# Two cross-attentions on one Trainium2 core: ScalarE rounds a key after it normalises probabilities instead of before

## The reference, cut to what matters

```python
def _cross_attention(q_in, kv_in, wq, bq, wk, bk, wv, bv, wo, bo, bias_k, bias_v):
    qh = (q_in @ wq + bq).reshape(b, q_len, H, K)          # 16 heads of 128
    kh = (kv_in @ wk + bk).reshape(b, t, H, K)
    vh = (kv_in @ wv + bv).reshape(b, t, H, K)
    kh = jnp.concatenate([kh, jnp.broadcast_to(bias_k, (b, 1, H, K))], axis=1)
    vh = jnp.concatenate([vh, jnp.broadcast_to(bias_v, (b, 1, H, K))], axis=1)
    logits = jnp.einsum('bqhk,bthk->bhqt', qh, kh) / jnp.sqrt(K)
    weights = jax.nn.softmax(logits, axis=-1)
    ctx = jnp.einsum('bhqt,bthk->bqhk', weights, vh).reshape(b, q_len, H * K)
    return ctx @ wo + bo
```

## Time and profile before

| | |
|---|---|
| median of 3 runs | 2650.89 us (2647.5 to 2654.44) |
| the profiled execution: its time, its span | 2650.34 us, 2648.6 us |
| PE busy | 2456.9 us, 93% of the span |
| PEld busy | 2163.3 us, 82% |
| DVE busy | 1382.3 us, 52% |
| ACT busy | 1133.2 us, 43% |
| POOL busy | 871.7 us, 33% |
| mean granted TensorE clock | 0.956 |

### The profile page before, as it was taken

One profiled execution on the slowest core, in us unless ns is written; L12 is line 12 of the kernel. 1 busy time (PEld: TensorE's weight loads), 2 busy tenths in 40 slices (PEclk: granted clock), 3 DMA queues, 4 the chain that ended last, 5 costly groups with the idle time before them and its releaser, 6 DMA issues. The chain is left out here.

```text
span 2648.6 us, 37894 instructions
## 1 busy us (share of the span) xinstructions
PE 2456.9 (93%) x13976; PEld 2163.3 (82%) x13976; DVE 1382.3 (52%) x2328; ACT 1133.2 (43%) x2441; POOL 871.7 (33%) x514
## 2 busy tenths in 40 slices
PE   7899689989999699899999999989998999999698
PEld 5676334479897467699999999989998999999698
DVE  4566631268886643232266666633335666664642
ACT  4677112123322332222476666622236566664320
POOL 1100322262210460252265454507216454542300
PEclk9899879989999699899999999999999999999799
DMA  7553263489995147344666655525266566653300
GB/s 234 128 137 72 77 220 113 113 246 229 249 235 183 68 158 242 120 157 155 203 220 201 196 188 176 172 74 208 106 228 218 167 198 199 198 186 107 123 9 25
DMA packets 196347, 432.94 MB, mean 163 GB/s; under 512 B 57820, under 2 KB 92660, under 8 KB 195396
## 3 DMA queue, kind: packets, MB, share of 16 engines
q1 hardware_dynamic: 196164, 430.52, 52.4%
HBM read 332.35 MB, written 106.27 MB: 166 GB/s over the span
## 5 line engine op out<-in xcount | busy, mean ns | idle before, releaser
L2008 PE MATMUL att_ring<-ca_pp,att_arena 128*128 128x400 f32 (+1 forms) x2304 | 431.3, 345 | 9.7 <-issue 7.5
L2008 PEld LDWEIGHTS att_ring<-ca_pp,att_arena 128*128 128x128 f32 (+1 forms) x2304 | 417.6, 189 | 16.0 <-issue 15.7
L2088 POOL TENSOR_TENSOR att_arena<-att_arena 128x1448 fp32r<-128x1448 f32 x64 | 212.2, 3316 | 471.8 <-ACT att_arena L2095 317.1
L2008 PE MATMUL att_ring<-att_arena,qk_wh 128*128 128x362 f32 x1024 | 256.0, 332 | 0.0
L2714 DVE TENSOR_TENSOR ca_yl<-att_ring,att_arena 128x400 fp32r<-128x400 f32 x256 | 146.7, 573 | 193.6 <-ACT att_arena L2675 193.6
L2008 PE MATMUL att_ring<-att_arena,qk_wl 128*128 128x362 f32 x512 | 173.0, 338 | 18.4 <-POOL att_arena L2275 17.8
L2008 PEld LDWEIGHTS att_ring<-att_arena,qk_wh 128*128 128x128 f32 x1024 | 185.3, 192 | 0.0
L2675 ACT ACTIVATE att_arena<-att_ring 128x400 fp32r<-128x400 f32 x256 | 129.0, 504 | 86.6 <-PE att_ring L2008 86.5
L2101 ACT ACTIVATE att_kstage<-att_score,att_shift 100x362 f32<-100x362 f32 x256 | 143.8, 563 | 43.4 <-DVE att_shift L2114 43.3
L1075 ACT ACTIVATE rec_stage<-rec_fbank,rec_columns 128x361 f32<-128x361 f32 x128 | 72.1, 564 | 196.4 <-PE rec_fbank L2008 195.6
L2008 PE MATMUL att_score<-att_arena 128*100 128x362 f32 x768 | 143.9, 337 | 0.8 <-POOL att_arena L2073 0.8
(11 more groups left out here) (410 smaller groups left out, 5898.4 us busy)
## 6 DMA issues: line engine op xcount, KB each, us to landing
att_arena<-ctx_parts SPq DMA_DIRECT2D x64, 1024.0 KB, 5.8
att_arena<-keys SPq DMA_DIRECT2D x64, 724.0 KB, 4.6
att_arena<-ctx_parts SPq DMA_DIRECT2D x64, 420.0 KB, 6.9
keys<-rec_stage SPq DMA_DIRECT2D x32, 724.0 KB, 4.2
keys<-att_kstage SPq DMA_DIRECT2D x32, 724.0 KB, 3.2
l_arena<-kept_value SPq DMA_DIRECT2D x176, 100.0 KB, 5.5
queries<-att_loose SPq DMA_DIRECT2D x64, 200.0 KB, 3.0
att_arena<-queries SPq DMA_DIRECT2D x64, 200.0 KB, 3.0
```

The lines of the kernel that those rows point to most:

```text
L2008: issued = nc.tensor.matmul(out, x, y, start=(first and k == 0), stop=(last and k == count - 1))
L2088: self.nc.gpsimd.tensor_tensor(self.kl[:, n % 2].bitcast(F32R), self.kl[:, n % 2], self.kh[:, n % 2].bitcast(F32), ALU.subtract).then_inc( ...
```

## The change

In each step ScalarE's four `normalise` of step n + 1 now stand ahead of `high_key(n + 3)`. Nothing is added or removed, and the lists of the other engines are as they were.

```diff
                 if n < STEPS:
                     for i in range(3):
                         turned_high(n, i)
-                if n + 3 < STEPS:
-                    t.high_key(act, n + 3)
                 if n + 1 < STEPS:
                     for h in range(G3):
                         t.normalise(act, n + 1, h)
+                if n + 3 < STEPS:
+                    t.high_key(act, n + 3)
                 j = half_due(n)
                 if j is not None:
```

## The result

The changed kernel takes 2671.01 us (median of 6 runs, 2667.57 to 2672.91) against 2650.61 us before (median of 6, those of the table above and three more). Its ratio to the kernel before is 1.0072, with a 95% interval of 1.0059 to 1.0084, so it is slower by some 19 us; the two medians differ by 20.4 us, the interval runs from 15.6 to 22.3 us. The forecast was 2667 us in a range of 2657 to 2673. The profiled execution took 2670.04 us, with a span of 2668.3 us and a mean granted clock of 0.956, as before.

What follows compares the result with a forecast made beforehand. TensorE's own list was taken to bound the steady part. 12.0 us from light steps and 4.4 us from the first steps made 16.4 us on 2650.34, 2666.7 us, forecast as 2667 us for the median, range 2657 to 2673.

Steps and rivals of the forecast that it cites:

- What bounds the kernel: Steady steps: TensorE's own list sets the pace; the split key and query lie ready only 2.02 us early.
- How much later the key comes: Light steps: key rounding starts 2.97 us later, against 2.02 us of slack, so the scores start 1.00 us late.
- How many steps: Steady part: 12 light steps over two attentions lose 1.00 us each, 12.0 us; the other steps cost nothing.
- The first four steps: Start of each attention, where DMAs are late: 2.2 us lost per attention, 4.4 us for both.
- Its larger term: Step 3 of the second attention: late key rounded 1.59 us later, 1.19 us lost; first attention taken as alike.
- The other term: Steps 0 to 2: GpSimd's weights split passes a net 1.0 us delay to step 2's key; bounds 0 and 1.5.
- step 1 starts earlier on ScalarE: Step 0's normalisation fits into ScalarE's idle time, so mixed contexts come 1.95 us earlier and step 1 starts earlier.
- The later mixed context costs nothing: Light step 7, ScalarE: first mixed context 1.02 us late, yet the exponential behind it could start at about 1412.03, before 1412.24.
- The clock: Rival: TensorE's clock falls in the 12 new gaps, 1.7 us each, 20 us more, 2687 us; chance 0.04.
- this rival's sign: The clock rival is decided by whether the scores behind the gap take over 3 us.
- The delay wasn't hidden: Rival: key rounding only 2 us later, light steps cost nothing, 2651 to 2655 us; chance 0.12.
- The gain by VectorE's earlier shift: Rival: shift 1.9 us sooner brings exponentials forward, 8 us gained, 2643 us; chance 0.03.

Runs made afterwards that it cites:

- e2: Kernel before, with normalising ahead of the key's rounding only in steps from n = 4 on that are not light; ratio 0.9994 (0.9983 to 1.0004).
- e4: Changed kernel, with GpSimd splitting the query ahead of the key; ratio to the kernel before 1.0001 (0.9992 to 1.0010).
- e5: Kernel before, with two of four normalisations ahead of the key's rounding; heads steps 18.98 or 18.99 us, one profiled execution 2656.89 us.
- e6: Kernel before, with three of four normalisations ahead of the key's rounding; heads steps 19.47 to 19.49 us, one profiled execution 2661.71 us.
- e3: Kernel before, with normalising ahead of the key's rounding only in steps 0 to 3 of each attention; ratio 1.0013 (1.0000 to 1.0027).
- e1: Kernel before, with normalising ahead of the key's rounding only in light steps n = 7, 11, ..., 27; ratio 1.0041 (1.0028 to 1.0055).

## Why the prediction was right

**What bounds the kernel.** Right. TensorE alone sets the pace of the steady steps, and the wait that came late was the one with the least slack, the split of key and query; e2 and e4 show it from both sides.

**How much later the key comes.** Right by each term: the normalisation starts 0.04 us behind the inversion's end (0.03 forecast), the rounding starts 2.98 us later in the step (2.97), and the scores 0.06 us behind the split's end (0.05). The loss for a heads step is 0.97 us where I had 1.00; the 2.98 less 2.02 of slack, plus the 0.06, would be 1.02, and the split itself was 0.05 us quicker than before (from 1416.25 to 1421.48, 5.23 us, against 5.28).

**How many steps.** Right: 12, and no others in the steady part, 11.6 us against 12.0. e5 and e6 show that the slack read from the rows was the real threshold.

**The first four steps.** The size, 4.4 us, is in line with e3 (3.4 us by the timing, 4.8 by means over profiles). Its larger term is borne out by the traces: step 3's late key was to cost 1.19 us, and the heads step behind it, step 4, lasts 20.18 us in the changed kernel's second attention and 20.19 us in both of e3, with TensorE idle for 0.97 us ahead of its scores. In the changed kernel's first attention step 4 lasts 19.83 us, and in the six attentions of the table where nothing is moved there 18.98 to 19.01. The other term, 1.0 us an attention in the steps ahead of it, is not shown: steps 0 to 3 together take 47.96 us as a mean of the four and 46.67 as a mean of the six, 1.3 us more, but they scatter by 1.9 us within the four and by 4.4 us within the six.

The working behind that second term held in part. Step 0 gets shorter, and TensorE gains nothing by it, as forecast: the scores of step 1 start 4.17 or 4.18 us into the step in the four attentions and 2.38 or 2.39 in the six, as they wait for GpSimd's split, which the earlier contexts don't bring forward. That "step 1 starts earlier on ScalarE" held in three attentions of four. Counted from TensorE's turning of step 0, ScalarE's first rounding of step 1 comes after 13.8 to 14.4 us in the first attentions where nothing is moved and 15.3 to 15.7 in the second ones; in e3 after 12.99 and 13.34, in the changed kernel after 14.52 and 14.54. The 14.52 is no gain, because there the rounding waits for the stacking of step 0's rows by DMA. ScalarE's timeline of that step:

```profile
1327.56 1.29 ACT L2669 ACTIVATE ca_pp<-att_ring 128x400 fp32r<-128x400 f32 x3 [1.93 <-DMA ca_extra<-ca_pp]
1329.75 2.06 ACT L2106 ACTIVATE att_kstage<-att_kstage,att_share 100x362 f32<-100x362 f32 x4 [0.90 <-DVE att_share L2119]
1331.72 1.40 ACT L2095 ACTIVATE att_arena<-att_arena 128x1448 fp32r<-128x1448 f32 x1
```

What ScalarE won by the reordering it spent here in waiting for that DMA, 1.93 us, so the key's rounding came 18.68 us behind the turning of step 0, where it was 14.96, and not 1.0 us later; the weights' split followed it. Two effects follow in this profile that my working didn't have. VectorE's shift of step 2 stood 4.35 us, under the weights' split, and ScalarE waited 2.37 us for it; the rows below are VectorE's, GpSimd's and ScalarE's of step 2. And SyncE's next stacking, which waits behind the same split, came late, so that ScalarE waited 2.69 us in step 3.

```profile
1342.42 4.35 DVE L2114 SCALAR_TENSOR_TENSOR att_shift<-att_top,att_zeros 100x4 f32<-100x4 f32 x1
```

```profile
1342.08 4.66 POOL L2649 TENSOR_TENSOR ca_wvl<-state_X,ca_wvh 128x2048 fp32r<-128x2048 f32 x1
```

```profile
1346.80 0.56 ACT L2101 ACTIVATE att_kstage<-att_score,att_shift 100x362 f32<-100x362 f32 x1 [2.37 <-DVE att_shift L2114]
```

Neither effect is shown to be the change's. In e1, which moves nothing in these steps, ScalarE waited longer still for the same shift, 6.01 us in step 2:

```profile
1340.91 6.96 DVE L2114 SCALAR_TENSOR_TENSOR att_shift<-att_top,att_zeros 100x4 f32<-100x4 f32 x1
```

```profile
1347.90 0.56 ACT L2101 ACTIVATE att_kstage<-att_score,att_shift 100x362 f32<-100x362 f32 x1 [6.01 <-DVE att_shift L2114]
```

And in e3's two attentions, which have the change in these steps, ScalarE doesn't wait for that shift in step 2; the wait for the stacking in step 3 is 1.91 and 1.46 us there, 1.32 us in the second attention before. How much of the loss each carries stays open.

**The later mixed context costs nothing.** Right: the exponential behind it starts 6.39 us into step 7 (1416.46 - 1410.07), before it was 6.60, and e2 has no loss in 38 steps that carry the same delay.

**The rivals.** The clock didn't fall in the 12 new gaps of the steady part: it is 1.00 in each of these heads steps. In the first steps it falls with and without the change: in step 1 it is 0.74 and 0.86 before and 0.88 and 0.78 after. One place there fits this rival's sign where it was 1.00 before. In step 3 of the first attention TensorE waits 1.94 us and the scores behind it take over 3 us; the granted clock of that step is 0.88.

```profile
1351.94 3.67 PE L2008 MATMUL att_score<-att_arena 128*100 128x362 f32 x12 [1.94 <-POOL att_arena L2073]
```

But in e1, which moves nothing there, the same step ran at 0.74, so this isn't shown to be the change's either. The delay wasn't hidden: the rounding came 2.98 us later and not 2. The gain by VectorE's earlier shift didn't come, though the shift did come 1.9 us earlier; VectorE's busy time fell from 1382.3 to 1295.1 us and nothing was won by it.

**The sum.** 11.6 us in the steady part and some 4 in the first steps make 15 to 16 us; e1 and e3 together give 14.3 us (0.41% and 0.13%), and e2 adds nothing to it. The two kernels' own comparison gives 19 us, with an interval of 15.6 to 22.3 us (0.59% to 0.84% of 2650.61), and I had 16.4. The parts lie at or just under its lower end. As e1 and e3 have intervals of some 3.6 us to each side themselves, the difference isn't shown to be real, and if it is, its cause is open.

## What to carry to other kernels

Where one engine is full, read for each thing it waits for how long it lay ready before it was taken. Here a delay cost nothing up to that slack and its full excess beyond. So a reordering that takes 3 us from the chain with 2 us to spare, to help the one with 4.5, is a loss in prospect, whatever idle time it removes. Ask too whether the work ahead in a list was only covering a wait: here the key's rounding ran while the inversion was awaited, and behind the reordering that time stood empty. And where a chain passes through a second engine, its order is a lever as well: splitting first what doesn't depend on the late input brought the changed kernel back to the time of the kernel before, and made that one 0.15% faster too. Last, before reading a difference between two profiles, look how far the same stretch differs where nothing was changed: that is how 8.6 us came down to about 4 here.

## What the runs showed of the hardware

That a four-column VectorE instruction can stand 2.08 us was in the trace before; that the same instruction stands 4.35 us where a longer GpSimd instruction covers it, and 0.16 us where none does, I hadn't expected to matter. It starts at 1342.42 and ends at 1346.77, 0.03 us behind the end of GpSimd's 4.66 us subtraction. The Trainium skill, SBUF — State Buffer, "SBUF: two separate sides", has it as an exclusive hold of the shared port pair for a whole instruction, and these rows agree with that. It can be more than one instruction: e1's shift of 6.96 us ends at 1347.87, 0.01 us behind the last of three GpSimd instructions that follow one another without a gap. Nor does the next GpSimd instruction always come first: in step 2 of the profile before, the shift took 0.35 us from 1343.39, to 0.01 us behind the end of one GpSimd instruction, though the next had started at 1343.68.

```profile
1339.12 4.69 POOL L2649 TENSOR_TENSOR ca_wvl<-state_X,ca_wvh 128x2048 fp32r<-128x2048 f32 x1
1343.76 3.29 POOL L2088 TENSOR_TENSOR att_arena<-att_arena 128x1448 fp32r<-128x1448 f32 x1
1347.00 0.86 POOL L2071 TENSOR_TENSOR att_arena<-att_arena,att_nothing 128x400 fp32r<-128x400 f32 x1
```

The other surprise is the scatter of the first steps, which wait for DMAs: the same five steps took 63.8 to 68.2 us, where steady heads steps repeat within 0.02 us, so two profiles tell the steady part's change and not the first steps'. The term for step 3 is an exception, as it shows in the length of step 4, which repeats to 0.03 us where nothing is moved.
